# Post-norm decoder layer on one core: low halves of the softmax shifts on GpSimd, and a new written order

## What is computed

```python
x = layernorm(x + self_attn(x, Wqkv, q_norm_w, k_norm_w, Wo))   # 16 heads of 32, RMS norm of q and k, rope, causal
x = layernorm(x + xattn(x, ctx, ctx))   # 8 heads of 64 features; softmax over the 512 feature columns
x = layernorm(x + ffn(x, weight))       # both operands rounded to fp8 in blocks of 128
```

## Time and profile before

| | |
|---|---|
| median of three runs | 2878.4 us |
| the profiled execution, its own time | 2875.41 us |
| its span, first to last instruction | 2873.7 us |
| busy share of the span | PE 93%, DVE 90%, ACT 78%, POOL 56% |
| DMA engines, mean busy share | 45.5% |
| mean granted TensorE clock | 0.984 of full speed |
| chain of work that ended last | PE 45%, DVE 24%, issue 11%, SP queue 10%, DMA 7% |

### The profile page before, as it was taken

How to read it: one execution, slowest core, us unless ns; L and a number is a source line. 1 busy time by engine, 2 the same in 40 slices (tenths; PEclk the granted TensorE clock), 3 DMA queues, 4 the chain that set the end, 5 groups by cost and what they waited for, 6 DMA issues and landing times.

```text
span 2873.7 us, 77579 instructions
## 1 busy us (share of the span) xinstructions
PE 2675.4 (93%) x20775; PEld 1347.1 (47%) x20775; DVE 2582.6 (90%) x4042; ACT 2244.6 (78%) x4039; POOL 1611.4 (56%) x2257
## 2 busy tenths in 40 slices
PE   5789999999999999999999999999999999999986
PEld 4554444445444444444444544444444444454321
DVE  7578999999999999999999999999999999998995
ACT  4457788888888888888888888888888888887765
POOL 3444655655655655555565665565555556555533
PEclk8799999999999999999999999999999999999998
...
DMA packets 382348, 396.92 MB, mean 138 GB/s; under 512 B 84417, under 2 KB 313793, under 8 KB 382145
## 3 DMA queue, kind: packets, MB, share of 16 engines
q1 hardware_dynamic: 382144, 394.95, 45.5%
...
## 4 chain that ended last, share of the span: by engine, by line
PE 45%; DVE 24%; issue 11%; SPq 10%; DMA 7%; POOL 1%; ACT 1%; DVEq 0%; POOLq 0%; ACTq 0%
PE psum L1647 10%; DVE nm L1327 10%; PE psum L1632 8%; PE psum L1488 7%; DMA xb<-x 6%; PE psum L1618 5%; PE psum L1481 3%; SPq L929 3%; PE psum L1542 3%; DVE sh L1334 2%; SPq L980 2%; DVE sh L1348 2%; PE psum L1663 2%; PE psum L1584 2%; PE psum L1664 2%
## 5 line engine op out<-in xcount | busy, mean ns | idle before, releaser
L1144 ACT ACTIVATE pp<-psum 128x512 f32<-128x512 f32 x2048 | 1146.5, 602 | 329.4 <-PE psum L1632 283.7
L1327 DVE TENSOR_REDUCE nm<-psum 128x2 f32<-128x1024 f32 x1024 | 1214.0, 1211 | 29.5 <-PE psum L1618 26.0
L1632 PE MATMUL psum<-qst,kst 98*128 98x512 f16 x2048 | 679.7, 386 | 13.3 <-DVE nm L1327 6.7
L1647 PE MATMUL psum<-pp,vT 128*17 128x512 f32 x4096 | 507.5, 597 | 0.4 <-ACT pp L1144 0.3
L1618 PE MATMUL psum<-kpair,qpair 64*128 64x512 bf16 x2048 | 361.9, 385 | 46.2 <-DVE nm L1327 36.2
L1488 PE MATMUL psum<-w_h,xT_h 128*128 128x512 f32 x768 | 387.0, 504 | 9.5 <-DVE xT_l L1356 6.0
L1067 POOL TENSOR_SCALAR_AFFINE_SELECT sm<-sm 128x512 f32<-128x512 f32 x256 | 163.0, 637 | 369.1 <-ACT sm L1187 368.9
L1632 PEld LDWEIGHTS psum<-qst,kst 98*128 98x128 bf16 x2048 | 169.2, 97 | 387.1 <-issue 232.1
L1488 PE MATMUL psum<-w_h,xT_l 128*128 128x512 f32 x768 | 307.7, 401 | 0.0
L1488 PE MATMUL psum<-w_l,xT_h 128*128 128x512 f32 x768 | 307.6, 401 | 0.0
L1618 PEld LDWEIGHTS psum<-kpair,qpair 64*128 64x128 f16 x2048 | 82.8, 93 | 385.3 <-issue 203.8
...
## 6 DMA issues: line engine op xcount, KB each, us to landing
qst<-q_rows SPq DMA_DIRECT2D x128, 320.0 KB, 3.7
kst<-k_rows SPq DMA_DIRECT2D x128, 320.0 KB, 3.6
kpair<-k_pair_rows SPq DMA_DIRECT2D x256, 128.0 KB, 3.0
qpair<-q_pair_rows SPq DMA_DIRECT2D x256, 128.0 KB, 2.9
...
```

Of the source, the lines that this page charges most:

```text
L1144: a.activation(pp[:, unit % 3, j, :], at(f"sc{n}"), ACT.Exp, scale=CROSS_SCALE).then_inc(st_free, 1)
L1327: v.tensor_reduce(cols, both(n), AX.X, ALU.max, negate=True).then_inc(mx_free, 1)
L1632: t.matmul(at(f"sc{n}"), kst[:, h, i * P:(i + 1) * P], qst[:, h, :], start=True, stop=True).then_inc(st_full, 1)
L1647: last = t.matmul(at(f"pv{g}")[32 * j:32 * j + XD + 1, :], vT[b.i][:, i, GROUPS * j + g, :], pp[:, unit % 3, j, :], start=(i == 0), stop=( ...
```

## The change

- `self_shift` and `cross_shift` keep only VectorE instructions that read `nm`: the quotient in f32 into a new buffer (`unit1`, `unit2`) and the same quotient in f16 (the high part). The `scalar_tensor_tensor` that made the low part is gone.
- The low part is a `tensor_tensor` subtraction on GpSimd (`self_low`, `shift_low`), in steps of their own.
- The turns are VectorE steps of their own, `self_turn` and `shift_turn`.
- `cross_max` 0 and 8 and `self_max` 0 also wait for the high part of the batch before.
- The steady tables, fills and drains of all five queues and the assignment of banks are new. For both groups of `cross_scores_T` all 32 parts now run in one slot; `shift_turn:0` comes in the slot after `cross_shift:0`.

The core of the diff. The tables of SP and POOL and DVE are whole, of ACT, PE and the banks what is spoken of; fills and drains are left out:

```diff
...
+        unit1, unit2 = sb("unit1", [P, NH]), sb("unit2", [P, GROUPS, 16])
...
         SP_STEPS = steps("""
-            ld_x:0@0 st_kpair:0@4 ld_kpair:0@4 st_sh1:0@1 ld_sh1:0@1 st_x2:0@2 st_kpl:0@4
-            st_qpl:0@2 ld_qst:0@5 ld_kpair:1@4 ld_qpair:1@4 ld_x2r:0@6 ld_kst:0@5 st_sh2:0@5
-            ld_sh2:0@5 st_qpair:0@2 ld_qst:1@5 ld_cx:0@3 st_sh2:1@5 ld_qpair:0@3 ld_kst:1@5
-            ld_sh2:1@5 st_out:0@7""")
+            ld_x:0@0 st_sh2:1@6 ld_x2r:0@7 st_kpair:0@4 st_qpl:0@3 ld_qst:1@6 ld_qpair:0@4
+            st_kpl:0@4 ld_kpair:0@4 st_sh1:0@1 st_x2:0@2 ld_kpair:1@4 ld_sh1:0@1 st_qpair:0@2
+            ld_kst:1@6 ld_sh2:1@6 ld_qpair:1@4 st_sh2:0@5 ld_kst:0@5 ld_cx:0@3 ld_qst:0@5
+            ld_sh2:0@5 st_out:0@7""")
         POOL_STEPS = steps("""
-            layer_rstd:0@2 quant_unit:0@7 mean_square:0@0 quant_round:0@7 rope_sum:0@0
-            mean_square:1@0 quant_round:1@7 part_low:0@0 query_low:0@2 mask:0@1 rope_sum:1@0
-            mask:1@1 part_low:1@0 mask:2@1 mask:3@1 causal:0@0 oT_low:0@1 layer_rstd:2@7
-            causal:1@0 cross_scale:0@6 cross_scale:1@6 add_cross:0@6 context_rest:0@3
-            context_rest:1@3 causal:2@0 layer_rstd:1@6 causal:3@0""")
+            cross_scale:1@7 self_low:0@1 add_cross:0@7 mean_square:0@0 query_low:0@2
+            layer_rstd:1@7 rope_sum:0@0 mean_square:1@0 part_low:0@0 mask:0@1 mask:1@1
+            quant_unit:0@7 rope_sum:1@0 mask:2@1 mask:3@1 part_low:1@0 shift_low:1@5
+            quant_round:0@7 quant_round:1@7 oT_low:0@1 causal:0@0 shift_low:0@4 causal:1@0
+            layer_rstd:2@7 context_rest:0@3 causal:2@0 context_rest:1@3 layer_rstd:0@1 causal:3@0
+            cross_scale:0@6""")
...
         ACT_STEPS = steps("""
...
+            self_probs:0@1 self_probs:1@1 probs:12@6 probs:13@6 probs:14@6 self_probs:2@1
+            self_probs:3@1 part_high:1@0 self_stack:1@0 self_stack:0@0 probs:15@6 self_stack:2@0
...
         DVE_STEPS = steps("""
-            cross_max:12@5 xT_low:0@0 cross_max:13@5 self_max:3@1 quant_scale:0@7 self_shift:0@1
-            cross_max:14@5 quant_magic:0@7 rope_terms:0@0 cross_shift:0@5 cross_max:15@5
-            cross_max:0@4 cross_max:1@4 cross_turn:0@6 rope_terms:1@0 cross_max:2@4 cross_max:3@4
-            cross_max:4@4 add_ffn:0@7 add_ffn:1@7 cross_max:5@4 cross_shift:1@5 cross_max:6@4
-            self_recip:0@1 add_ffn:2@7 self_norm:0@1 add_ffn:3@7 self_max:0@0 cross_max:7@4
-            cross_turn:1@6 cross_max:8@4 self_max:1@0 back_turn:0@6 cross_max:9@4 cross_max:10@4
-            add_self:0@1 cross_max:11@4 cross_stats:0@6 self_max:2@0""")
+            xT_low:0@0 cross_max:12@5 self_max:3@1 cross_turn:1@7 self_shift:0@1 cross_max:13@5
+            back_turn:0@7 self_turn:0@1 shift_turn:0@5 cross_max:14@5 cross_max:15@5
+            cross_stats:0@7 rope_terms:0@0 cross_shift:1@5 cross_max:0@4 cross_max:1@4
+            cross_max:2@4 quant_scale:0@7 rope_terms:1@0 cross_max:3@4 quant_magic:0@7
+            cross_max:4@4 cross_max:5@4 self_recip:0@1 shift_turn:1@5 self_norm:0@1 cross_max:6@4
+            cross_turn:0@6 cross_max:7@4 add_ffn:0@7 self_max:0@0 add_ffn:1@7 add_ffn:2@7
+            cross_shift:0@4 add_ffn:3@7 cross_max:8@4 self_max:1@0 add_self:0@1 cross_max:9@4
+            self_max:2@0 cross_max:10@4 cross_max:11@4""")
         PE_STEPS = steps("""
...
+            x_T:0@0 cross_scores:12@5 cross_pv:7@7 cross_scores_T:0@6 cross_scores_T:1@6
+            proj_q:0@0 proj_q:1@0 cross_scores:13@5 cross_scores_T:2@6 cross_scores_T:3@6
+            proj_q:2@0 cross_scores_T:4@6 cross_scores_T:5@6 proj_q:3@0 cross_scores:14@5
...
+            cross_scores:2@4 cross_scores_T:11@6 proj_v:3@0 self_scores_T:0@1 self_scores_T:1@1
+            cross_scores_T:12@6 cross_pv:0@6 cross_scores:3@4 cross_scores_T:13@6 parts_T:0@0
+            cross_scores_T:14@6 self_scores_T:2@1 self_pv:0@1 self_pv:1@1 self_scores_T:3@1
+            cross_scores:4@4 cross_pv:1@6 cross_scores_T:15@6 parts_T:1@0 cross_scores:5@4
...
+            ffn:3@7 self_scores:1@0 proj_o:1@1 cross_scores:8@4 cross_scores_T:23@6
+            cross_scores_T:24@6 cross_scores_T:25@6 cross_scores_T:26@6 proj_o:2@1 proj_o:3@1
+            cross_scores_T:27@6 self_scores:2@0 cross_scores_T:28@6 cross_scores_T:29@6
+            cross_scores:9@4 cross_pv:4@6 cross_pv:5@6 cross_scores_T:30@6 cross_scores_T:31@6
+            cross_scores:10@4 self_scores:3@0 cross_scores:11@4 cross_pv:6@6""")
...
-        SC_BANK = "74507562465430305602602232324721"
-        MX_BANK = "01 45 56 01 45 56 56 34 12 67 12 01 12 56 12 56"
+        SC_BANK = "32032033622774551030127705107537"
+        MX_BANK = "34 56 34 23 23 23 23 45 23 12 01 23 01 56 45 12"
...
 
+            def shift_low(b, g):
+                pool.wait_ge(s_h2, b.n(GROUPS, g + 1))
+                g_.tensor_tensor(sh2[:, g, 1, :], unit2[:, g, :], sh2[:, g, 0, :], ALU.subtract).then_inc(s_l2, 1)
+
+            def self_low(b, _):
+                pool.wait_ge(s_h1, b.n(1, 1))
+                g_.tensor_tensor(sh1[:, 1, :], unit1[:], sh1[:, 0, :], ALU.subtract).then_inc(s_l1, 1)
...
@@ -1323,30 +1333,36 @@
             def cross_max(b, n):
                 dve.wait_ge(mx_full, b.n(N_MX, n + 1))
                 p, c = n // KC, n % KC
+                if n % (PG * KC) == 0:
+                    dve.wait_ge(s_h2, b.n(GROUPS, p // PG + 1 - GROUPS))
                 cols = nm2[:, p // PG, :].rearrange("m (l q c) -> m l q c", l=PG, q=2)[:, p % PG, :, c]
                 v.tensor_reduce(cols, both(n), AX.X, ALU.max, negate=True).then_inc(mx_free, 1)
 
             def cross_shift(b, g):
 
                 dve.wait_ge(mx_free, b.n(N_MX, N_MX // GROUPS * (g + 1)))
+                v.tensor_scalar(unit2[:, g, :], nm2[:, g, :], 1.0 / SHIFT_UNIT, None, ALU.mult)
                 v.tensor_scalar(sh2[:, g, 0, :], nm2[:, g, :], 1.0 / SHIFT_UNIT, None, ALU.mult).then_inc(s_h2, 1)
-                dve.wait_ge(s_h2, b.n(GROUPS, g + 1))
-                v.scalar_tensor_tensor(sh2[:, g, 1, :], nm2[:, g, :], 1.0 / SHIFT_UNIT, sh2[:, g, 0, :],
-                                       ALU.mult, ALU.subtract).then_inc(s_l2, 1)
+
+            def shift_turn(b, g):
+
                 dve.wait_ge(s_l2, b.n(GROUPS, g + 1))
                 dve.wait_ge(d_sh2_stored[g], b.n(16, 0))
                 v.transpose(sh2T[g][:], sh2[:, g].rearrange("p a r -> p (a r)")).then_inc(s_sh2[g], 1)
 
             def self_max(b, c):
                 dve.wait_ge(s_causal, b.n(KC, c + 1))
+                if c == 0:
+                    dve.wait_ge(s_h1, b.n(1, 0))
                 v.tensor_reduce(nm1[:, HC * c:HC * (c + 1)], sm[:], AX.X, ALU.max, negate=True).then_inc(s_max1, 1)
 
             def self_shift(b, _):
                 dve.wait_ge(s_max1, b.n(KC, KC))
+                v.tensor_scalar(unit1[:], nm1[:], 1.0 / SHIFT_UNIT, None, ALU.mult)
                 v.tensor_scalar(sh1[:, 0, :], nm1[:], 1.0 / SHIFT_UNIT, None, ALU.mult).then_inc(s_h1, 1)
-                dve.wait_ge(s_h1, b.n(1, 1))
-                v.scalar_tensor_tensor(sh1[:, 1, :], nm1[:], 1.0 / SHIFT_UNIT, sh1[:, 0, :],
-                                       ALU.mult, ALU.subtract).then_inc(s_l1, 1)
+
+            def self_turn(b, _):
+
                 dve.wait_ge(s_l1, b.n(1, 1))
                 dve.wait_ge(d_sh1_stored, b.n(16, 0))
                 v.transpose(sh1T[:], sh1[:].rearrange("p a h -> p (a h)")).then_inc(s_sh1, 1)
```

More of the change, by code:

```diff
@@ new lines, in post_ln_decoder_kernel @@
+            ld_x:0/0 ld_w:0-5/0 ld_consts:0/0 ld_cx:0/0 ld_wo:0/0 ld_wf:0/0 ld_x:0/1 st_sh1:0/0
+            ld_sh1:0/0 st_kpair:0/0 ld_x:0/2 st_sh1:0/1 ld_sh1:0/1 st_x2:0/0 st_qpair:0/0 ld_x:0/3
+            ld_qpair:0/0 st_qpl:0/0 ld_qpair:1/0 st_x2:0/1 ld_kpair:0/0 st_sh1:0/2 ld_sh1:0/2
+            st_qpl:0/1 st_qpair:0/1 ld_x:0/4 st_kpl:0/0 st_sh1:0/3 ld_sh1:0/3 ld_cx:0/1
+            ld_kpair:1/0 st_x2:0/2 ld_x:0/5 st_qpair:0/2 st_kpair:0/1 ld_qpair:0/1 ld_kpair:0/1
+            st_sh1:0/4 st_sh2:0/0 st_qpl:0/2 ld_sh1:0/4 ld_qpair:1/1 st_kpl:0/1 st_x2:0/3
@@ new lines, in post_ln_decoder_kernel @@
+            ld_cx:0/2 ld_kpair:1/1 ld_qst:0/0 ld_kst:1/0 ld_kst:0/0 ld_qpair:0/2 ld_sh2:0/0
+            ld_qst:1/0 st_qpair:0/3 st_qpl:0/3 st_sh2:1/0 ld_x:0/6 st_kpair:0/2 ld_kpair:0/2
+            ld_qpair:1/2 st_sh1:0/5 ld_sh1:0/5 ld_sh2:1/0 st_x2:0/4 ld_kpair:1/2 st_kpl:0/2
+            ld_x2r:0/0 ld_kst:0/1 st_qpl:0/4 st_sh2:0/1 ld_qpair:0/3 ld_qst:0/1 ld_cx:0/3
+            ld_sh2:0/1 ld_x:0/7 st_sh2:1/1 st_qpair:0/4 st_kpair:0/3 ld_kpair:0/3 st_x2:0/5
+            ld_kst:1/1 st_sh1:0/6 ld_sh1:0/6 st_qpl:0/5 ld_qst:1/1 ld_sh2:1/1 st_kpl:0/3
@@ new lines, in post_ln_decoder_kernel @@
+            ld_qst:0/2 ld_cx:0/4 ld_qpair:1/3 st_sh2:0/2 ld_kpair:1/3 ld_kst:0/2 st_qpair:0/5
+            ld_x:0/8 ld_qpair:0/4 ld_sh2:0/2 st_kpair:0/4 ld_x2r:0/1 st_x2:0/6 st_sh1:0/7
+            ld_kpair:0/4 ld_sh1:0/7 st_sh2:1/2 ld_sh2:1/2 st_out:0/0 ld_kst:1/2 ld_qst:1/2
```

(7 more changed lines are left out.)

885 lines of the change are left out of this document (426 added, 459 removed), and 10 rows, old and new, of the table BANK.

## The result

| us | before | changed |
|---|---|---|
| median of the runs (6 each, side by side) | 2877.41 (2870.08 to 2880.97) | 2885.55 (2881.77 to 2892.66) |
| the profiled execution, own time / span | 2875.41 / 2873.7 | 2881.77 / 2880.0 |
| start to the 6th `add_self` | 254.2 | 249.7 |
| 55 slots, 6th to 61st `add_self` | 2336.8 | 2323.2 |
| 61st to the last (64th) `add_self` | 128.3 | 123.5 |

The ratio is 1.0037 with a 95% interval of 1.0026 to 1.0049: slower by 8 us, where 78 us of gain were forecast. The starts of `add_self` say where the 6.3 us of span come from: -4.5 at the front, -13.6 and -4.8 in the loop, +29.2 at the end. The last row is the odd one: one slot in two has the forecast length, 41.15 us. The slot behind each loop branch is 1.9 us longer.

What follows compares the result with a forecast made beforehand. DVE was taken as the bound, PE close behind. DVE at 40.2 us plus 0.9 of mutual waits gave a 41.1 us slot, 1.37 less over 57 slots: 78 us off 2875.4, 2797, median 2800 us; range 2735 to 2866.

Steps and rivals of the forecast that it cites:

- the sum's assumption that a slot is a slot: Steady loop and its ends: 57 full-length slots, each 1.37 us shorter, together 78 us saved.
- PE's wait falls to about 0.2: PE ahead of `x_T`: its wait for the load of x falls from 1.41 us through more work after `proj_o:3`.
- Fill and drain: Both ends of the run, reordered too: counted as 0 us, within 15 either way.
- Shift steps on DVE: `self_shift` and `cross_shift` groups, turns included: 3.9 us per slot falls to 1.2, saving 2.7 if no stall returns.
- 0.4 us returned by stalls: Shift `tensor_scalar` on DVE sometimes held by GpSimd: 0.4 us per slot given back, leaving 2.3 net.
- rival 1: Shift `tensor_scalar` pairs stall on GpSimd as the low parts did; 0.6 us per slot remains, about 2844 us; chance 0.17.
- GpSimd +0.2 each: Three added 128x16 subtractions per slot on GpSimd: 0.2 us each, hidden in POOL's 17.4 us idle per slot.
- Turns at nothing: `self_turn` and `shift_turn` as own DVE steps, later than their shifts: no cost if the low part is ready.
- rival 3: DVE waits at `shift_turn:1` for GpSimd's late low part; one microsecond costs 57 us, about 2932 us; chance 0.12.
- Slot 41.1: Steady loop: DVE at 40.2 us per slot plus 0.9 for two near-full engines waiting on each other.
- Rival 2: DVE's gain misses what sets the slot: the `proj_o`, `add_self`, load, `x_T` chain or PE holds it; about 2872 us; chance 0.13.
- Wrong altogether: Sign of failure: a slot at or above 42.5 us without the other signs, from a wait the new order makes elsewhere.

Runs made afterwards that it cites:

- e3: The changed kernel with 64 always-fulfilled waits put ahead of SP's loop: 2822.47 us, ratio 0.9812 to the kernel before.
- e18: The kernel before with 192 padding waits (96 instructions) ahead of ACT's loop: 2870.36 us, ratio 0.9974.
- e6: e3 with the low parts made on DVE again, turns still own steps, GpSimd's two new steps left out: 2895.01 us, ratio 1.0063 to the kernel before.
- e7: e3 with `quant_magic` one `cross_max` later, away from `rope_sum:1`: 2829.65 us, ratio 0.9834 to the kernel before.

## Why the prediction failed

**Sign and size.** Forecast for the profiled execution was 2797 us, measured 2881.8: 85 us more. e3 splits this: its 2822.5 is the changed kernel without the stall. So about 59 us are the stall, 56 of them in the 55 slots (2323.2 to 2267.0), which is 25 slots longer by 1.9 and six of these by another 1.5. The other 25 are the end (+26.6), the front (-5.5) and the loop, which saved 69.8 + 4.2 = 74 of the 78 forecast (+4).

**The step that failed** is the sum's assumption that a slot is a slot: "the full-length slots are the 52 of the loop and some five at its ends", all at one length, got by adding up PE and DVE. What an engine does at the branch was in no term. The load of x was looked at ("PE's wait falls to about 0.2", by better cover), and this held in every second slot. The sentence on SP ("no transfer is added") counted the steps in the queue, but not the queue's own instructions. A hint was in the trace before: slots of 42.79 and 42.08 in turn, in a table that repeats exactly. A steady table whose slots differ by 0.7 us says that something depends on the round; the forecast averaged it away to 42.47. e18 shows that about 0.45 of the 0.7 was ACT's fetches.

**Fill and drain "0, within 15 either way"** was the second failure: -4.5 and +29.2 (+26.6 in e3). The zero had no row behind it. What could have been counted is the work that the new table leaves to the end, by its stages: all 32 `cross_scores_T` and `probs` of a batch now run six turns behind, where 5 and 9 of them ran five behind, and `cross_pv:7`, `cross_turn:1`, `back_turn` and `add_cross` seven instead of six. That this makes the 15 us is likely, not shown.

**Shift steps on DVE: right.** The four lines are at 110 to 167 ns on average, none stalled in the loop; the two instructions of a group start 0.07 and 0.08 us apart where I looked (900.53 and 900.61, 920.83 and 920.90). e6 shows the removed part's price.

**0.4 us returned by stalls: mis-sized and misplaced.** No shift instruction is caught in the loop. `quant_magic` is, by 1.10 us per slot (1207 + 738 against 418 + 428). DVE's busy time per slot fell from 39.6 to 38.4 (1155.58 / 1238 x 41.15), not to 37.3 as 2.3 saved would have it. The timeline of the changed kernel shows the collision:

```profile
907.52 1.27 POOL L1059 TENSOR_TENSOR ropeA<-ropeA,ropeB 128x512 f32<-128x512 f32 x1
...
907.87 1.21 DVE L1450 TENSOR_SCALAR yc<-yq 128x512 int32<-128x512 int32 x1
...
908.75 1.59 POOL L1075 TENSOR_SCALAR_AFFINE_SELECT p<-p 128x512 f32<-128x512 f32 x2
...
909.11 0.74 DVE L1453 TENSOR_SCALAR yc<-yc 128x512 f32<-128x512 f32 x1
```

The first ends 0.29 us after `rope_sum`; its own work is 0.42. The second begins under GpSimd's `mask`, an `affine_select`, and ends 0.28 us after the first of the two. It is so in 53 and 54 of the 64 batches. In the kernel before the first mostly ran beside a GpSimd `tensor_tensor` of one column (L1043) and wasn't held (418 ns). This is rival 1's mechanism at a line that it didn't name. The Trainium skill (SBUF — State Buffer, section Who interferes with whom) lists `tensor_scalar` among the operations that can take the shared pair of ports, and this row agrees. What it costs in time no run shows in full: e7 gave back 0.2 us of it and the slot didn't move, and DVE has 2.7 us of a slot free.

**GpSimd +0.2 each: right** (0.22). **Turns at nothing: right**; DVE idles 1.7 us in the whole run for POOL ahead of `self_turn` and not at all ahead of `shift_turn`, so rival 3 (`shift_turn:1` waits for GpSimd) did not happen.

**Slot 41.1: right without the stall** (41.15), and so was the guess that two near-full engines pay 0.9 on top of a DVE of 40.2, but for the wrong reason: PE alone is busy for 40.8 of it (1226.39 / 1238 x 41.15). Unless that busy time holds waits of its own, the count of 39 us of PE work was too low.

**Rival 2** named an end near the measured one (2872) through the chain of the x load, with PE waiting. It has the right victim, but supposed a full chain in every slot. The chain isn't too long: it is started late in every second slot. "Wrong altogether: a wait that the new order makes elsewhere" is nearest to what came (the mean slot is 42.24, in turn 43.05 and 41.15), though not made by the order of the steps but by the number of instructions ahead of and in SP's loop.

Three sums of the prediction are slightly off and decide nothing: rival 1's 2.0 of 2.7 leaves 0.7 us per slot and not 0.6; in SP's table nine steps stand ahead of `st_sh1`, not seven; `part_low:1` ends 3.8 us after `rope_terms:1`, not 3.9.
